# One transformer block on one core: three scatters moved ahead of the root, and the shared expert's first two chunks moved later

## The reference

```python
# 1. mix the four groups: softmax weights per image and token from a small MLP
h = einsum('bgcd,gbc->bcd', x, softmax(gelu(mean(sum_g x)) @ w1.T + b1) @ w2.T + b2)
# 2. causal attention per image, 16 heads of 16 channels
h = h + (softmax(causal(Q K^T) / 4) V) @ W_o.T + b_o        # Q, K, V from layernorm(h)
# 3. mixture of experts on x = layernorm(h), 2048 tokens
shared = silu(x @ sg_w.T) * (x @ su_w.T) @ sd_w.T
scores = sigmoid(x @ gate_w.T) + gate_bias                  # 64 experts in 8 groups
# the 4 best groups, in them the 6 best experts, their scores normalised to sum 1
routed = sum over the 6 experts: weight * (silu(x @ eg.T) * (x @ eu.T)) @ ed.T
h = h + shared + routed
```

## Time and profile before

| What | Value |
|---|---|
| median of three runs | 561.03 us (559.43 to 562.28) |
| the profiled execution, its own time | 560.77 us |
| its span in the profile | 559.0 us |
| PE busy | 472.0 us (84%) |
| DVE busy | 340.1 us (61%) |
| ACT busy | 281.2 us (50%) |
| POOL busy | 252.8 us (45%) |
| granted TensorE clock, mean | 0.941 of full speed |

### The profile page before, as it was taken

The page is one execution under the profiler, slowest core; times in us unless marked ns, Lnnn a source line. Parts: engine busy times, 40 slices in busy tenths (PEclk is TensorE's granted clock), DMA queues, the critical chain, the costliest instruction groups (busy, mean ns, idle before and its releaser), DMA issues. The chain is left out here.

```text
span 559.0 us, 12585 instructions
## 1 busy us (share of the span) xinstructions
PE 472.0 (84%) x2990; PEld 355.2 (64%) x2991; DVE 340.1 (61%) x1054; ACT 281.2 (50%) x910; POOL 252.8 (45%) x277
## 2 busy tenths in 40 slices
PE   0466899999999999987679999999999999997923
PEld 0343676777776766654437787787787787783522
DVE  3715367998999999887753343443443444441797
ACT  2257478877788887871113444444454454441000
POOL 1100111466666666666741546555565565544000
PEclk9967689999999999997899999999999999998967
DMA  8999920011111111121234568557577746542996
GB/s 270 346 333 288 284 60 2 30 67 69 68 59 58 58 66 68 71 75 68 105 110 121 187 190 276 166 170 236 173 211 214 222 143 207 178 150 92 414 360 251
DMA packets 57589, 91.04 MB, mean 163 GB/s; under 512 B 7911, under 2 KB 44650, under 8 KB 57552
## 3 DMA queue, kind: packets, MB, share of 16 engines
q1 hardware_dynamic: 44880, 62.41, 36.9%
q0 software_dynamic: 10368, 26.07, 13.0%
q10 hardware_dynamic: 2304, 2.10, 1.1%
HBM read 87.09 MB, written 41.60 MB: 230 GB/s over the span
## 5 line engine op out<-in xcount | busy, mean ns | idle before, releaser
L392 POOL DMA_INDIRECT y_rows<-y,xring x120 | 118.0, 984 | 108.0 <-issue 67.1
L1021 PE MATMUL ps<-wring,prob 128*128 x480 | 124.5, 382 | 9.1 <-ACT prob L543 9.1
L970 DVE TENSOR_TENSOR probt<-probt,ps 128x128 f32<-128x128 f32 x120 | 34.5, 287 | 119.2 <-ACT probt L548 108.5
L1021 PEld LDWEIGHTS ps<-wring,prob 128*128 128x128 f32 x480 | 81.8, 190 | 17.6 <-issue 11.5
L450 ACT ACTIVATE prob<-ps,nmax 128x128 f32<-128x128 f32 x256 | 69.6, 388 | 5.1 <-DVE nmax L676 3.9
L1021 PE MATMUL ps<-wring,probt 128*128 x240 | 72.0, 382 | 0.0
L548 ACT ACTIVATE probt<-ps 128x128 f32<-128x128 f32 x120 | 33.3, 277 | 71.4 <-PE ps L1021 71.4
L543 ACT COPY prob<-ps 128x256 f32<-128x256 f32 x121 | 45.0, 373 | 47.4 <-PE ps L1236 44.8
L978 DVE TENSOR_SCALAR y<-ps,xring 128x256 f32<-128x256 f32 x120 | 57.8, 483 | 6.4 <-PE ps L1021 4.1
L365 POOL DMA_INDIRECT slot_rows<-row,slot_ix x48 | 52.7, 1097 | 13.7 <-issue 13.4
L365 POOL DMA_INDIRECT slot_rows<-xring,slot_ix x48 | 51.0, 1062 | 14.0 <-issue 14.0
(11 more groups left out here) (177 smaller groups left out, 779.6 us busy)
## 6 DMA issues: line engine op xcount, KB each, us to landing
wring<-wexp SPq DMA_DIRECT2D x121, 384.0 KB
xring<-slot_rows SPq DMA_DIRECT2D x121, 129.0 KB, 2.1
x_sb<-y_rows SPq DMA_DIRECT2D x16, 768.0 KB, 7.3
slot_rows<-pads SPq DMA_DIRECT2D x1, 8256.0 KB, 36.5
x_sb<-x SPq DMA_DIRECT2D x3, 2048.0 KB, 17.8
slot_rows<-pads SPq DMA_DIRECT2D x5, 516.0 KB, 10.3
x_sb<-x SPq DMA_DIRECT2D x4, 512.0 KB, 5.9
out<-h_all ACTq DMA_DIRECT2D x16, 128.0 KB, 6.9
```

The lines of the kernel that those rows point to most:

```text
L392: nc.gpsimd.indirect_dma_start(out=y_dram, out_offset=bass.IndirectOffsetOnAxis(ap=xring[:, q, TO_AT:TO_AT + 1].bitcast(I32), axis=0), in_ ...
L970: nc.vector.tensor_tensor(hm[:, q % 2, :], silu[:, q % 2, :], psS[q % 2][:, INTER:2 * INTER], ALU.mult).then_inc(S("h_ready"), 1)
L1021: return nc.tensor.matmul(*a, **k)
```

## The change

Four things are done.

1. POOL issues the first three scatters of image b-3 ahead of the roots of step b, and the other three behind them.
2. The parts of chunk 0 move: part 0 from behind the transposes of step 16 to behind its projection, part 2 from ahead of the gate product of step 17 to behind it, part 3 into step 18. The down product leaves the steps and stands behind the table's products. The gate is one Silu on ACT in place of a tanh and a DVE instruction, for all chunks.
3. Chunk 1 moves from the turn to behind the tiles, where its result stays in PSUM as that of chunks 2 and 3. The products of the next two chunks stand at iterations 8 and 13 of DVE's last loop (before: chunk 3's at iteration 5).
4. The table's first product waits for the count of the last image (`counted`, `key_read`) and no longer for its finished rows (`row_ready`).

```diff
@@ POOL, step
-                if -2 < b <= NB:
+                if has(e):
+                    pool.wait_ge(S("row_ready"), e + 1)
+                    pool.sem_inc(S("pool_step"), 1)
+                    scatter(range(0, 3))
+                if -2 < b <= NB:
                     pool.wait_ge(S("var_ready"), b + 4 if b < 0 else 2 * b + 4 if b <= 12 else b + 16)
                     roots(0 if has(b + 3) else 1, 2 if has(b - 1) else 1, b + 3)
                 if has(e):
-                    pool.wait_ge(S("row_ready"), e + 1)
-                    pool.sem_inc(S("pool_step"), 1)
-                    scatter(range(TOPK))
+                    scatter(range(3, TOPK))
@@ ACT
-            def shared_tanh(j):
+            def shared_silu(j):
...
-                    nc.scalar.activation(sth[:, m, :], psG[m][:], ACT.Tanh, scale=0.5).then_inc(S("gu_tanh"), 1)
+                    nc.scalar.activation(sth[:, m, :], psG[m][:], ACT.Silu).then_inc(S("gu_silu"), 1)
...
-            shared_tanh(1)
...
-            for j in range(2, 4):
+            for j in range(1, 4):
+                shared_silu(j)
@@ DVE
                     nc.vector.tensor_tensor(selsum[:, 0:E], selsum[:, 0:E], sel_b[:, q, :], ALU.add).then_inc(
-                        S("d_chain"), 1)
+                        S("counted"), 1)
...
             def shared_mul(j):
                 for m in range(2):
+                    dve.wait_ge(S("gu_silu"), 2 * j + m + 1)
                     dve.wait_ge(S("gu_done"), 4 * j + 3 + m)
-                    dve.wait_ge(S("sh_mul"), 2 * j + m + 1)
                     wait(dve, S("shared_done"), 4 * (j - 1))
-                    nc.vector.scalar_tensor_tensor(out=sht[:, j % 2, m, :], in0=sth[:, m, :], scalar=0.5,
-                                                   in1=psU[m][:], op0=ALU.mult, op1=ALU.mult).then_inc(
+                    nc.vector.tensor_tensor(sht[:, j % 2, m, :], sth[:, m, :], psU[m][:], ALU.mult).then_inc(
                         S("sh_chain"), 1)
@@ DVE, steps 17 and 18
-                if isinstance(b, int) and b == NB + 1:
-                    shared_gate(0)
-                    shared_mul(0)
-                if isinstance(b, int) and b == NB + 2:
-                    shared_out(0)
@@ DVE, behind the table
-            shared_gate(1)
-            shared_mul(1)
-            shared_out(1)
+            shared_mul(0)
+            shared_out(0)
@@ DVE, the end
-            late_mul(2)
+            shared_mul(1)
             for b in range(NB + 2):
-                if b == 5:
-                    late_mul(3)
+                if b in (8, 13):
+                    shared_mul(2 + b // 13)
...
-                    if b - 1 < NB // 2:
+                    if b - 1 < 4:
                         dve.wait_ge(S("h2_ready"), b)
@@ PE
-            FIRST_CHUNK = {(NB, 1): 0, (NB, 3): 1, (NB + 1, 1): 2, (NB + 1, 2): 3, (NB + 2, 1): 4}
+            FIRST_CHUNK = {(NB, 2): 0, (NB, 3): 1, (NB + 1, 2): 2, (NB + 2, 1): 3}
...
-            pe.wait_ge(S("row_ready"), NB)
+            pe.wait_ge(S("counted"), NB)
+            pe.wait_ge(S("key_read"), NB)
...
-            shared_up(1, 0)
             pe.wait_ge(S("t_rows"), 1)
...
-            shared_up(1, 1)
             pe.wait_ge(S("t_rows"), 2)
...
-            shared_up(1, 2)
-            shared_up(1, 3)
-            shared_down(1)
+            shared_down(0)
             pe.wait_ge(S("tab_ready"), TABLES)
-            pe.wait_ge(S("h2_ready"), 8)
+            pe.wait_ge(S("h2_ready"), 4)
...
             for m in range(4):
-                late_up(2, m)
-            late_up(3, 0)
-            late_up(3, 1)
-            late_down(2)
-            late_up(3, 2)
-            late_up(3, 3)
-            late_down(3)
+                late_up(1, m)
+            for j in range(1, 4):
+                if j < 3:
+                    late_up(j + 1, 0)
+                    late_up(j + 1, 1)
+                late_down(j)
+                if j < 3:
+                    late_up(j + 1, 2)
+                    late_up(j + 1, 3)
```

More of the change, by code:

```diff
@@ L222, in build @@
                      "x2_transposed", "x2t_ready", "gate_done", "gate_tanh", "g_chain", "score_read", "sel_ready",
-                     "pos_done", "key_read", "d_chain", "pool_step", "gu_done", "gu_tanh", "sh_chain", "sh_mul",
+                     "pos_done", "key_read", "d_chain", "pool_step", "gu_done", "gu_silu", "sh_chain", "counted",
                      "shared_done", "h2_ready", "row_ready", "t_chain", "t_count", "t_cum", "t_past", "t_rows",
@@ L527, in step @@
                 if isinstance(b, int) and b == NB + 1:
-                    shared_tanh(0)
+                    shared_silu(0)
             image_loop(act, step, -2, NB + 1)
-            shared_tanh(1)
             act.wait_ge(S("tab_ready"), TABLES)
@@ L554, in _ @@
             tile_loop(act, SCALAR, tile_step, -1, 1)
-            for j in range(2, 4):
-                for m in range(2):
-                    act.wait_ge(S("gu_done"), 4 * j + m + 1)
-                    wait(act, S("sh_chain"), 2 * (j - 1) + m + 1)
-                    nc.scalar.activation(sth[:, m, :], psG[m][:], ACT.Silu).then_inc(S("gu_tanh"), 1)
+            for j in range(1, 4):
+                shared_silu(j)
             for b in range(NB):
@@ L758, in place @@
                 elif k == 2:
-                    dve.wait_ge(S("d_chain"), 2)
+                    dve.wait_ge(S("d_chain"), 1)
                     nc.vector.max(key8[:], key[:]).then_inc(S("d_chain"), 1)
                 elif k == 3:
-                    dve.wait_ge(S("d_chain"), 3)
+                    dve.wait_ge(S("d_chain"), 2)
                     nc.vector.tensor_scalar(slot_ix[:, d % NROW, :], key8[:, 0:TOPK], 1.0, None, ALU.subtract)
@@ L768, in place @@
                 elif k == 5:
-                    dve.wait_ge(S("d_chain"), 4)
+                    dve.wait_ge(S("d_chain"), 3)
                     nc.vector.tensor_tensor(wjunk[:], wjunk[:], masked[:, q, 0:E].unsqueeze(1).to_broadcast([P, TOPK, E]),
@@ L772, in place @@
                 elif k == 6:
-                    dve.wait_ge(S("d_chain"), 5)
+                    dve.wait_ge(S("d_chain"), 4)
                     nc.vector.reduce_sum(wraw[:], wjunk[:], axis=AX).then_inc(S("d_chain"), 1)
                 elif k == 7:
-                    dve.wait_ge(S("d_chain"), 6)
+                    dve.wait_ge(S("d_chain"), 5)
                     nc.vector.tensor_scalar(row_of(d)[:, :, W_AT:W_AT + 1].rearrange("p k o -> p (k o)"), wraw[:],
                                             tinv[:, q:q + 1], None, ALU.mult).then_inc(S("row_ready"), 1)
-            def shared_gate(j):
-                for m in range(2):
-                    dve.wait_ge(S("gu_tanh"), 2 * j + m + 1)
-                    nc.vector.scalar_tensor_tensor(out=sth[:, m, :], in0=sth[:, m, :], scalar=1.0, in1=psG[m][:],
-                                                   op0=ALU.add, op1=ALU.mult).then_inc(S("sh_mul"), 1)
             def shared_mul(j):
                 for m in range(2):
+                    dve.wait_ge(S("gu_silu"), 2 * j + m + 1)
                     dve.wait_ge(S("gu_done"), 4 * j + 3 + m)
-                    dve.wait_ge(S("sh_mul"), 2 * j + m + 1)
                     wait(dve, S("shared_done"), 4 * (j - 1))
-                    nc.vector.scalar_tensor_tensor(out=sht[:, j % 2, m, :], in0=sth[:, m, :], scalar=0.5,
-                                                   in1=psU[m][:], op0=ALU.mult, op1=ALU.mult).then_inc(
+                    nc.vector.tensor_tensor(sht[:, j % 2, m, :], sth[:, m, :], psU[m][:], ALU.mult).then_inc(
                         S("sh_chain"), 1)
@@ L981, in _ @@
             tile_loop(dve, VECTOR, tile_step, 0, 2)
-            def late_mul(j):
-                for m in range(2):
-                    dve.wait_ge(S("gu_tanh"), 2 * j + m + 1)
-                    dve.wait_ge(S("gu_done"), 4 * j + 3 + m)
-                    dve.wait_ge(S("shared_done"), 4 * (j - 1))
-                    nc.vector.tensor_tensor(sht[:, j % 2, m, :], sth[:, m, :], psU[m][:], ALU.mult).then_inc(
-                        S("sh_chain"), 1)
-            late_mul(2)
+            shared_mul(1)
             for b in range(NB + 2):
-                if b == 5:
-                    late_mul(3)
+                if b in (8, 13):
+                    shared_mul(2 + b // 13)
                 if b < NB:
@@ L1057, in shared_up @@
             def shared_up(j, m):
-                if j:
-                    if m < 2:
-                        pe.wait_ge(S("sh_mul"), 2 * (j - 1) + m + 1)
-                    else:
-                        pe.wait_ge(S("sh_chain"), 2 * (j - 1) + m - 1)
                 pe.wait_ge(S("x2t_ready"), 4 * j + 4)
@@ L1075, in shared_down @@
                          lambda k: sd_sb[:, k, :]).then_inc(S("shared_done"), 1)
-            FIRST_CHUNK = {(NB, 1): 0, (NB, 3): 1, (NB + 1, 1): 2, (NB + 1, 2): 3, (NB + 2, 1): 4}
+            FIRST_CHUNK = {(NB, 2): 0, (NB, 3): 1, (NB + 1, 2): 2, (NB + 2, 1): 3}
```

(10 more changed lines are left out.)

## The result

| | before | changed |
|---|---|---|
| time, median of 20 runs each | 560.8 us (555.9 to 562.6) | 563.77 us (559.2 to 565.1) |
| ratio, 95% interval | | 1.0048 [1.0026, 1.0071] |
| profiled execution, own time and span | 560.77, 559.0 | 564.82, 563.2 |
| mean granted clock | 0.941 | 0.944 |

The changed kernel is 3 us slower (the interval allows 1.5 to 4); I had forecast 9 us faster.

What follows compares the result with a forecast made beforehand. Bounds: DVE in the image steps, TensorE in the tiles, DMA engines at the end; no engine full in the turn. Steps -1.5, turn -5.7, end -1.8 sum to -9.0 us: 552.0 us, range 548 to 555.5 (8 in 10: 546.5 to 558.5).

Steps and rivals of the forecast that it cites:

- The image steps: Image steps: three scatters fit ahead of the root, the gsel line is freed of the bias add; -1.5 us.
- behind a start delay of 0.3 us (taken like the gap): Image steps: after row_ready the first scatter starts 0.3 us later; three end at 3.8 us, 0.6 before the root.
- 0.47 would be absorbed by DVE's wait in front of line 701: Image steps: if the moved bias add delays the mixing, DVE's wait hides 0.47 us, leaving 0.3 a step.
- its whole 0.74 us: Image steps: the most the moved bias add could hold up the mixing instruction, line 667.
- my first rival: Image steps: bias add or scatters hold DVE every step, +0.3 us in ten steps instead of -1.5; 556.5 us, chance 0.15.
- The turn: Between steps and tiles: first tile starts at about 291.7, not 297.45; -5.7 us, between -8 and -3.
- The tiles: Tile stage: nearly no loads in hand, but SP issues a tile's in 1.4 us against 1.78 needed; nothing charged.
- The end: Behind the tiles: DVE's stop at iteration 5 goes, lost transfer time returns; -1.8 us, between -3 and +2.
- The rival with TensorE as the bound of the end: Behind the tiles: none of TensorE's added 12 us is hidden, kernel slower at 565.8 us; chance 0.08.

Runs made afterwards that it cites:

- e5: Changed kernel without POOL's bias add (attention output's bias left out of the result): 553.53 us, ratio 0.9887.
- e6: Kernel before without POOL's bias add (attention output's bias left out of the result): 557.24 us, ratio 0.9947.
- e3: Changed kernel with two scatters ahead of the root and four behind, instead of three and three: 555.17 us, ratio 0.9913.
- e9: Kernel before with SP's first tile load held until the second image of the shared expert's chunk 1: 565.37 us, ratio 1.0106.
- e1: Changed kernel with no split, all six scatters behind the roots again: 556.72 us, ratio 0.9936.
- e14: Kernel before with SP's first tile load held until the first image of the shared expert's chunk 1: 565.11 us, ratio 1.0056.
- e11: Changed kernel with two scatters ahead of roots only from step 13 on, bias add waiting for the first score maximum before step 13: 551.19 us, ratio 0.9847.
- e8: Changed kernel with the split in step 16 alone, TensorE held before the first tile until tile 3 is loaded: 559.52 us, ratio 0.9971.

## Why the prediction was wrong

**The image steps: forecast -1.5, measured +9.1 at the root of step 14 (243.29, now 252.34).** This is the step that failed: I had three scatters fit ahead of the root, and the bias add cost no more in its new place than it gained in the old. That three scatters end 3.8 us after `row_ready`, "behind a start delay of 0.3 us (taken like the gap)", is wrong by 0.5 us: 0.30 is the gap between scatters that follow one another, and an idle POOL needs 0.82. This alone makes the root late by 0.17 us a step (e5 against e6), and it eats the leg in which the gain of 0.21 lay. And "0.47 would be absorbed by DVE's wait in front of line 701" holds only while DVE sets that leg, as in e3; with three scatters POOL sets it. I also charged the bias add with "its whole 0.74 us" against one instruction; it slowed two, by 0.92 together. The mechanism itself was my first rival, with 0.15 and a price of +0.3 us a step; it came at +0.91.

**The turn: forecast -5.7, measured -6.0 from the root of step 14 to the first transpose (54.2, now 48.2 us).** Right, in the sum and in most of its parts. (From the root of step 14 to the last scatter are 2.3 of the 6.0 us, so that the +6.7 above is the steps' 9.1 less these.) With the 9.1 us of the steps taken off, the last scatter stands at 283.7 (forecast 283.5 to 285.0), the end of the table at 283.4 (282.5 to 284), SP's first load at 287.5 (287.2 to 288.7), the end of the down product at 290.9 (290 to 293) and the first transpose at 291.5 (291.7). The root of step 15 came 2.1 us late for the 1.6 forecast, which the twelve scatters behind it did not follow. The table's chain took some 8.3 us for the 7.5 that I had reckoned.

**The tiles: "so I charge nothing", measured +3.2.** I compared SP's rate with TensorE's and took the 7 us in hand as unneeded. A rate says nothing of the single slow load: 2.1 us of the loss are TensorE's two waits for such loads; the rest is open.

**The end: forecast -1.8, measured -2.1.** Right, and the trace agrees with the reason given, though no run isolates it: DVE's stop at iteration 5 is gone, no window from 525 to 555 falls under 406 GB/s, and the added TensorE work of a chunk lies mostly in its former wait of 10.48 us. The rival with TensorE as the bound of the end did not happen: its granted clock was 1.00 from 525 to 560.

Added up, -9.0 became +4.2, and the difference of 13.2 us is: steps 10.6 (+9.1 for -1.5), turn -0.3, tiles 3.2, end -0.3. These terms are read from single profiled executions. Kernels with the unsplit step of 12.68 us reach one and the same root between 127.0 (e9) and 130.1 us (before), so a term that starts at 0 can be off by some 3 us; the step itself is a difference within one execution and repeats within 0.01 us. The medians put the split at 6 to 7 us.

## What to carry to other kernels

A gap between instructions that follow one another is not what an idle engine needs to start: look in the trace for the same instruction behind a wait. Before counting a wait as room for a delay, write the step as a loop of legs and ask which engine sets the leg that holds the wait; if the change fills this leg with another engine's work, neither the room nor a saving there is left. When GpSimd work is moved, list the VectorE instructions that it will stand beside: the four with two SBUF inputs here grew by 0.4 to 0.6 us each beside a bias add of 0.74 us, and one with a single SBUF input, the gsel line, by 0.21. And a loop whose loads come faster on average than it uses them can still wait for a single slow one: compare the lead with the slowest load, not with the mean.

## What the runs showed of the hardware

- An indirect scatter on an idle GpSimd started 0.82 us behind the end of what released it (182.62 to 183.44), against 0.30 behind another scatter. The trace of before held it, in a row that I had not read for this: the y scatter at 510.75 waited for a DVE instruction that began at 509.39 and takes 0.48, so it started 0.88 us behind its end:

```profile
510.75 0.98 POOL L392 DMA_INDIRECT y_rows<-y,xring  x1 [1.95 <-DVE y L978]
```
- Beside a 128x256 bias add on GpSimd, VectorE instructions with two SBUF inputs took 0.98 for 0.48, 1.12 for 0.55, 0.97 for 0.56 and 0.60 for 0.18 us, and the gsel line, with one SBUF input, 0.38 for 0.17. The bias add itself took 1.09 for 0.74 us beside two of them in a row. The two with a PSUM input kept their 1.28 and 0.41 us.
- TensorE behind an idle stretch of 4.4 us (e1) did its first tile's products in 2.07 us for 1.03, half the clock, though the granted clock stood at 1.00 while it sat idle; behind 2.9 us (e9) it did the same, and behind 0.9 us in e14 and 1.5 us in e11 it took 1.13. A wait put in to gain a lead (e8) costs this way too.
